# Attention times V as three passes into one PSUM bank, one group of three tiles, a second attention with P as weights, and a written-out tail

## The reference

```python
B, Q, S, D, H, DH = 8, 100, 1444, 128, 16, 64
def first(x, ctx):                       # wq, wk, wv, wo, norm_w are weights
    normed = x * rsqrt(mean(x*x, -1) + 1e-6) * norm_w
    q, k, v = heads(normed @ wq), heads(ctx @ wk), heads(ctx @ wv)
    return x + merge(softmax(q @ k.T) @ v) @ wo
def second(x1, ctx):
    return x1 + softmax(x1 @ ctx.T) @ ctx
out = second(first(x, ctx_1024), ctx_1024)
```

## Time and profile before

| what | value |
|---|---|
| median of 3 runs | 704.48 us (704.47 to 707.13) |
| span of the profiled execution | 704.5 us |
| the profiled execution's own time | 706.28 us |
| PE busy | 680.9 us (97%) |
| PE weight loads busy | 604.9 us (86%) |
| DVE busy | 484.0 us (69%) |
| ACT busy | 469.5 us (67%) |
| POOL busy | 159.9 us (23%) |
| mean granted TensorE clock | 0.985 |

### The profile page before, as it was taken

One profiled execution on the slowest core, in us unless ns is written; L12 is line 12 of the kernel. 1 busy time (PEld: TensorE's weight loads), 2 busy tenths in 40 slices (PEclk: granted clock), 3 DMA queues, 4 the chain that ended last, 5 costly groups with the idle time before them and its releaser, 6 DMA issues.

```text
span 704.5 us, 13025 instructions
## 1 busy us (share of the span) xinstructions
PE 680.9 (97%) x4424; PEld 604.9 (86%) x4424; DVE 484.0 (69%) x1074; ACT 469.5 (67%) x1176; POOL 159.9 (23%) x486
## 2 busy tenths in 40 slices
PE   5899999999999999999999999999999999999976
PEld 5688889888998898988998889988999888988965
DVE  3586567677776777677776777677776777668722
ACT  4777577677766677667766677667776677666622
POOL 2211114111231214121241213221231212312100
PEclk9999999999999999999999999999999999999995
DMA  5012112120222111221121111211112112110120
GB/s 186 1 53 16 7 11 54 9 15 9 15 53 16 15 5 19 53 15 9 7 58 14 13 12 12 58 11 15 5 18 52 15 9 15 13 11 10 11 18 3
DMA packets 27146, 16.61 MB, mean 24 GB/s; under 512 B 15786, under 2 KB 25418, under 8 KB 27082
## 3 DMA queue, kind: packets, MB, share of 16 engines
q1 hardware_dynamic: 27082, 15.79, 17.0%
HBM read 15.32 MB, written 0.46 MB: 22 GB/s over the span
## 4 chain that ended last, share of the span: by engine, by line
PE 91%; DMA 3%; ACT 3%; DVE 2%; issue 1%; SPq 0%; ACTq 0%
PE ps_o L1072 31%; PE ps_t L1020 19%; PE ps_s L989 11%; PE ps_s L993 10%; PE ps_s L990 10%; PE ps_m L1088 4%; PE ps_m L931 3%; DMA denominator_rows<-rinv 2%; PE ps_t L945 2%; ACT probs L696 1%; DMA x_rows<-in_x_dram 1%; DVE pT_both L753 1%; PE ps_s L918 1%; DMA out_dram<-result 0%; DMA rinv_row<-denominator_rows 0%
## 5 line engine op out<-in xcount | busy, mean ns | idle before, releaser
L675 ACT ACTIVATE pT_both<-ps_t 128x496 fp32r<-128x496 f32 (+1 forms) x336 | 194.4, 581 | 188.4 <-PE ps_t L1020 188.0
L1072 PE MATMUL ps_o<-pT_both,c_hi 128*128 128x496 f32 (+4 forms) x768 | 253.3, 375 | 0.0
L753 DVE TENSOR_TENSOR pT_both<-ps_t,pT_both 128x496 fp32r<-128x496 f32 (+1 forms) x336 | 202.6, 616 | 45.4 <-ACT pT_both L675 44.9
L808 DVE TENSOR_REDUCE part_max<-ps_s 124x1 f32<-124x512 f32 (+1 forms) x336 | 209.2, 650 | 23.7 <-PE ps_s L993 23.5
L696 ACT ACTIVATE probs<-ps_s,neg_max 124x512 f32<-124x512 f32 (+1 forms) x336 | 218.9, 663 | 6.9 <-DVE neg_max L815 6.9
L1020 PE MATMUL ps_t<-ident,probs 124*128 124x124 f32 (+2 forms) x1232 | 184.3, 268 | 7.2 <-DVE pT_both L753 4.9
L1020 PEld LDWEIGHTS ps_t<-ident,probs 124*128 124x128 f32 (+2 forms) x1232 | 148.6, 141 | 46.4 <-issue 9.2
L1072 PE MATMUL ps_o<-pT_both,c_lo 128*128 128x248 f32 (+3 forms) x704 | 187.0, 266 | 0.0
L1072 PEld LDWEIGHTS ps_o<-pT_both,c_hi 128*128 128x128 f32 x768 | 146.6, 191 | 14.9
L539 POOL CAST tails<-probs 124x36 fp32r<-124x36 f32 (+1 forms) x224 | 41.0, 215 | 469.2 <-ACT probs L696 373.9
L989 PE MATMUL ps_s<-cT_hi,q_hi 128*124 128x512 f32 (+3 forms) x312 | 143.9, 461 | 1.2 <-DVE q_lo L753 1.2
(11 more groups left out here) (119 smaller groups left out, 493.0 us busy)
## 6 DMA issues: line engine op xcount, KB each, us to landing
rinv_row<-denominator_rows SPq DMA_DIRECT2D x48, 124.0 KB, 3.6
ctx_raw<-in_ctx_dram SPq DMA_DIRECT2D x8, 704.0 KB
denominator_rows<-rinv SPq DMA_DIRECT2D x48, 1.0 KB
wq_sb<-in_L_xattn_wq_dram SPq DMA_DIRECT2D x2, 256.0 KB, 5.8
wk_sb<-in_L_xattn_wk_dram SPq DMA_DIRECT2D x2, 256.0 KB, 6.0
wv_sb<-in_L_xattn_wv_dram SPq DMA_DIRECT2D x1, 512.0 KB, 7.7
wo_sb<-in_L_xattn_wo_dram SPq DMA_DIRECT2D x1, 512.0 KB, 8.7
rinv_row<-denominator_rows SPq DMA_DIRECT2D x8, 62.0 KB, 3.8
```

Source lines behind the costliest of these rows:

```text
L675: act.activation(pT_both[buf][:, j0:j0 + nj, 0, col:col + m], ps_t[:, bank, 0:nj * m].rearrange("p (j m) -> p j m", m=m), ACT.Copy).then_i ...
L753: dve.tensor_tensor(dst, src, hi.bitcast(F32), ALU.subtract).then_inc(done, 1)
L808: mx = dve.tensor_reduce(part_max[0:m, s, c:c + 1], ps_s[0:m, score_bank(s, c, par), 0:CHUNKS[c][1]], AX.X, ALU.max)
L1072: t = pe.matmul(*all_[i], start=(i == 0), stop=(i == len(all_) - 1))
```

## The change

It does these things at once:

- PV of a group runs as three passes per slot, c_hi x p_hi, c_hi x p_lo and c_lo x p_hi, all of the group's own width and all accumulated into one bank region: 34 matmuls for each group. DVE multiplies it by `rinv_row` straight into `o_norm` (`take_out`); the copy on ACT, the sum on DVE and the product on POOL go.
- The groups are (0,1), (2,3), (4,5), (6,7), (8,9,10), (11,12), and the plan of PV over the steps is new.
- The late PV has the transposed exponentials as weights (100 columns) and c_hi, c_lo side by side as the moving operand; its output has queries as rows, and the transpose back goes. ACT scales one half, POOL adds the x1 rows, DVE does the rest. It runs in one piece in step 12.
- The context is split in steps 13, 0 and 1 and stacked in step 2. The projection moves from steps 2 to 5 to steps 0 to 3, the q pairs to steps 5 to 10, 12 and 13, and the first item of every batch waits for all eight pairs.
- The late item of batch 6 is taken out of batch 7, and the end is written out: it runs there beside the last PVs of batch 7. The last group's denominators are spread over the partitions by a matmul with ones against diagonal matrices instead of the way over DRAM.

The diff, cut to its core:

```diff
-    GROUPS = [(0, 1), (2, 3), (4, 5), (6, 7), (8,), (9, 10), (11, 12)]
+    GROUPS = [(0, 1), (2, 3), (4, 5), (6, 7), (8, 9, 10), (11, 12)]
-    PV_PLAN = {0: (5, -1, 1, 2), 1: (6, -1, 0, 2), 2: (6, -1, 1, 2),
-               3: (0, 0, 0, 2), 4: (0, 0, 1, 2), 5: (1, 0, 0, 2), 6: (1, 0, 1, 2),
-               7: (2, 0, 0, 2), 8: (2, 0, 1, 2), 9: (3, 0, 0, 2), 10: (3, 0, 1, 2),
-               11: (LATE, -1, 0, 1), 12: (4, 0, 0, 1), 13: (5, 0, 0, 2)}
+    PV_PLAN = {13: (4, 0, 0, 17), 0: (4, -1, 17, 34), 1: (5, -1, 0, 17), 2: (5, -1, 17, 34),
+               3: (0, 0, 0, 17), 4: (0, 0, 17, 34), 5: (1, 0, 0, 17), 6: (1, 0, 17, 34),
+               7: (2, 0, 0, 12), 8: (2, 0, 12, 23), 9: (2, 0, 23, 34),
+               10: (3, 0, 0, 17), 11: (3, 0, 17, 34)}
+    LATE_PV_STEP = 12
+    EVAC = {1: (4, -1), 3: (5, -1), 5: (0, 0), 7: (1, 0), 10: (2, 0), 12: (3, 0)}
-    PAIR_STEPS = {1: 0, 6: 1, 7: 2, 8: 3, 9: 4, 10: 5, 13: 6}
-    LAST_PAIR_STEP = 0
+    PAIR_STEPS = {5: 0, 6: 1, 7: 2, 8: 3, 9: 4, 10: 5, 12: 6, 13: 7}
-    OUT_HEADS = {2: range(0, 5), 3: range(5, 9), 4: range(9, 13), 5: range(13, 16)}
+    OUT_HEADS = {0: range(0, 5), 1: range(5, 9), 2: range(9, 13), 3: range(13, 16)}
-    CTX_SPLIT_STEPS = {12: (0, 1), 13: (1, 1), 0: (2, 0)}
-    STACK_STEP = 1
+    CTX_SPLIT_STEPS = {13: (0, 1), 0: (1, 0), 1: (2, 0)}
+    STACK_STEP = 2
...
+            for b in range(B):                                  # SP
+                if b < B - 1:
+                    sp.wait_ge(ctx_turned, n(b, NC, NC - 1))
+                    sp.wait_ge(ctx_lo_done, n(b, len(CTX_SPLIT), len(CTX_SPLIT) - 1))
+                    sp.wait_ge(stack_steps, n(b, 3, 2))
+                    load_ctx(b + 1)
+                for g in range(NG):
...
+                    sp.wait_ge(inverted, k + 1)
+                    sp.dma_start(scratch[b:b + 1, cols].rearrange("a (t p) -> p (a t)", p=TM),
...
+                    sp.wait_ge(rinv_stored, 16 * (k + 1))
...
+                    sp.dma_start(rinv_row[:, k % 2, 0:TM * count],
...
+                    if (b, s) in NUMBER:                        # POOL
+                        split_tail(NUMBER[b, s])
...
+                    if s == STACK_STEP and 0 < b:
+                        stack_tail(b)
...
+            def late_scaled(bb):                                # ACT
+                act.wait_ge(pv_done, block(bb, LATE))
...
+                act.activation(late_lo[0:Q, :], ps_o[0:Q, 0, D:2 * D], ACT.Copy,
+                               scale=rinv[0:Q, k:k + 1]).then_inc(late_lo_out, 1)
...
+            def take_out(b, g):                                 # DVE
+                k, w = NG * b + g, group_width(g)
+                dve.wait_ge(pv_done, block(b, g))
...
+                    dve.wait_ge(rinv_row_loaded[g], 16 * (b + 1))
...
+                dve.tensor_tensor(o_norm[:, group_cols(g)], ps_o[:, 0, 0:w], rinv_row[:, k % 2, 0:w],
+                                  ALU.mult).then_inc(pv_out, 1)
...
+                    if s in EVAC:
+                        grp, off = EVAC[s]
+                        if b + off >= 0:
+                            take_out(b + off, grp)
+                    if here:
+                        chunk_maximum(g, 0)
...
+                    if s == 0:                                  # PE, scores
+                        pe.wait_ge(ctxT_lo, n(b, NC, NC - 1))
+                        pe.wait_ge(q_lo_done, pairs_up_to(b - b % 2, HP - 1))
...
+            def pv(b, grp, lo, hi, by_chunk=False):
...
+                    if block(b, grp) > 1:
+                        pe.wait_ge(pv_out, block(b, grp) - 1)
+                    if grp == 0:
...
+                        pe.wait_ge(ctx_lo_done, n(b, len(CTX_SPLIT), len(CTX_SPLIT) - 1))
+                        pe.wait_ge(stack_steps, n(b, 3, 2))
+                for i in range(lo, hi):
+                    j, part = divmod(i, 3)
...
+                    weights = c2[:, j, (0, 0, 1)[part], :]
+                    moving = p[:, j, (0, 1, 0)[part], 0:w]
+                    t = pe.matmul(ps_o[:, 0, 0:w], weights, moving, start=(i == 0), stop=(i == UNITS - 1))
...
+                    pe.matmul(ps_o[0:Q, 0, 0:2 * D], pT_late[:, j, 0, :],
+                              c2[:, j, :, :].rearrange("p a d -> p (a d)"), start=(j == 0), stop=False)
+                    pe.matmul(ps_o[0:Q, 0, 0:D], pT_late[:, j, 1, :], c2[:, j, 0, :],
+                              start=False, stop=False)
...
+            last = B - 1                                        # PE, the end
+            scores(L_FIRST, 0)
+            turn(T_LAST, 0)
+            scores(L_FIRST, 1)
+            turn(T_LAST, 1)
+            scores(L_FIRST, 2)
+            pv(last, NG - 2, 17, UNITS)
+            turn(T_LAST, 2)
...
+            project(last, range(0, 9))
...
+            pv(last, NG - 1, 0, UNITS, by_chunk=True)
+            project(last, range(9, 13))
+            turn(L_FIRST, 0)
+            turn(L_FIRST, 1)
...
+            project(last, range(13, 16))
+            turn(L_FIRST, 2)
...
+                scores(L_LAST, c)
...
+            pv_late(last - 1)
+            for c in range(NC):
+                turn(L_LAST, c)
+            pv_late(last, by_chunk=True)
```

More of the change, by code:

```diff
@@ L102, in n, with block @@
+    BLOCKS += [(B - 2, LATE), (B - 1, LATE)]
+    def block(b, g):
+        return BLOCKS.index((b, g)) + 1
+    TURNS = []
+    for g, (b, s, _, _) in enumerate(ITEMS):
+        if g > 0 and g < L_FIRST:
+            TURNS += [("item", g - 1, c) for c in range(NC)]
+        if b < B - 1 and s in CTX_T_STEPS:
+            TURNS.append(("ctx", b + 1, CTX_T_STEPS.index(s)))
+    for g in (T_LAST, L_FIRST, L_LAST):
+        TURNS += [("item", g, c) for c in range(NC)]
     def n(b, per_batch, index):
@@ L303, in bass_two_cross_attentions @@
-        TURNS = []
-        for s in range(STEPS):
-            TURNS += [("item", s - 1, c) for c in range(NC)]
-            if s in CTX_T_STEPS:
-                TURNS.append(("ctx", s, CTX_T_STEPS.index(s)))
-        def turn_exists(at, first, last, nxt):
-            what, s, _ = TURNS[at]
-            if what == "ctx":
-                return nxt
-            if s < 0:
-                return not first
-            return item_exists(s, first, last)
-        def turn_bank(what, s, c, par):
-            return (len(TURNS) * par + TURNS.index((what, s, c))) % 2
@@ new lines, in wait_turn_bank, with turn @@
+            def wait_turn_bank(what, at, c):
+                k = TURNS.index((what, at, c)) - 2
+                if k >= 0:
+                    what, at, c = TURNS[k]
+                    if what == "ctx":
+                        pe.wait_ge(ctxT_lo, n(at, NC, c))
+                    else:
+                        pe.wait_ge(turned_lo, ev(at, c))
+            def turn(g, c):
+                m = rows(ITEMS[g][2])
+                pe.wait_ge(exped, ev(g, c))
+                wait_turn_bank("item", g, c)
+                if g == 0 and c == 1:
+                    pe.wait_ge(wqk_ready, 4)
+                j0, nj = TILE_SLOTS[c]
+                for j in range(j0, j0 + nj):
+                    if j < FULL:
+                        src = probs[g % 2][0:m, P * j:P * (j + 1)]
+                    else:
+                        pe.wait_ge(tail_split, g + 1)
+                        src = tails[g % 2][0:m, :]
+                    t = pe.transpose(ps_t[:, turn_bank("item", g, c), m * (j - j0):m * (j - j0 + 1)], src,
+                                     ident[0:m, 0:m])
+                t.then_inc(turned, 1)
@@ new lines, in _ @@
+            for b in range(B):
+                for s in range(STEPS):
+                    here = (b, s) in NUMBER
+                    g = NUMBER.get((b, s))
+                    prev = item_before(b, s)
+                    part = pv_of(b, s)
+                    for c in range(NC):
+                        if here:
+                            scores(g, c)
+                        if prev is not None and c < NC - 1:
+                            turn(prev, c)
+                    mid = None
+                    if part is not None:
+                        bb, grp, lo, hi = part
+                        mid = lo + (hi - lo) // 2
+                        pv(bb, grp, lo, mid)
+                    if prev is not None:
+                        turn(prev, NC - 1)
+                    if part is not None:
+                        pv(bb, grp, mid, hi)
+                    if s == LATE_PV_STEP and 0 < b < B - 1:
+                        pv_late(b - 1)
+                    misc(b, s)
+                    if s in CTX_T_STEPS and b < B - 1:
@@ new lines, in _ @@
+            last = B - 1
[6 more added lines that the diff above has]
+            turn(T_LAST, 2)
+            pe.wait_ge(x1_rows_ready, last)
+            wait_heads(last, range(0, 9))
+            project(last, range(0, 9))
+            pe.wait_ge(diag_made, 2)
+            col = 0
+            for i, t in enumerate(GROUPS[NG - 1]):
+                m = rows(t)
```

(3 more changed lines are left out.)

1131 lines of the change are left out of this document (511 added, 620 removed).

## The result

The changed kernel takes 742.3 us (median of 4 runs, 739.6 to 744.5), the kernel before in the same session 705.3 us (704.5 to 707.1): a ratio of 1.053, with an interval from 1.051 to 1.055. The forecast was 719 us with a range from 700 to 728. The direction was right; the loss is 37 us where 14.5 were forecast.

A forecast was written before the change was run, and what follows sets the result against it. PE was taken as the bound, busy for 97% of the span. 704.5 - 5.0 (PV) + 10.1 (stack) + 13.2 (DMA) + 4.2 (pair 7) - 8.1 (end) = 718.9, say 719 us, range 700 to 728.

The forecast's parts named there:

- The DMA term: Group (0,1) denominators, stored behind the late context load, make PE wait before PV (2,3) in six batches: +13.2 us.
- three waits: New PE waits: stack before PV (0,1), 7 times; DVE's product behind the DMA, 6 times; pair 7, 3 times.
- PV on PE: PV and late PV in new passes save about 0.5 and 0.25 us a batch: -5.0 us.
- The rival of slow passes: Passes of 248 and 236 columns run at 0.125 us: 15 us more, 734 us; chance 0.06.
- the rule on loads: Skill's rule: weight loads overlap only across row groups, so 43 added loads a batch cost in full: 758 us; chance 0.01.
- The stack: Context's rest, stacked in step 2, is late for PV (0,1) in step 3: 1.4 us in batches 1 to 7, +10.1.
- Pair 7: First scores of batches 2, 4 and 6 wait for the last q pair: 1.4 us each, +4.2 us.
- The end: Written-out end of 33.5 us, 0.4 for batch 7's step 12, and a shorter batch 7: -8.1 us.
- The gain without waits: Rival: stack, row and pairs are all in time, so no wait arises: 691 us; chance 0.14.
- The row in time with the stack late: Rival: the stack is late but the DMA isn't, with a store of 5 to 6 us: 706 us; chance 0.09.

The follow-up runs named there:

- the kernel without the three waits: Changed kernel with the stack back in step 1, tiles waiting only for needed q pairs, and group (0,1) denominators stored and loaded before the next context: 700.6 us.
- the run with the product first: Kernel with all three waits removed, and DVE at the end taking out the last group before the late item's first two low parts: 698.2 us, ratio 0.989.
- the one with the row first: Changed kernel, but SP waits until the row of group (0,1) has landed before storing group (1)'s denominators: 745.5 us, ratio 1.055.

## Why the prediction was right or wrong

Two steps failed. The DMA term had the row's landing and the cost behind a wait too small: 26 us where it had 13.2. And the new plan was put at nothing away from its three waits, while each batch takes 0.5 us more instead of 0.75 less: +3 where the sum had -5.0. The three waits themselves, their places and their numbers (7, 6 and 3) came as forecast.

- **PV on PE (-5.0).** The prices of the passes inside a piece hold: 0.115 and 0.170 us, and the group of three takes 6.0 us where (8) and (9,10) took 6.7. The rival of slow passes (734) and the rule on loads (758) fall. But the gain did not arrive. In the kernel without the three waits, an even batch takes 79.75 us, before 79.71, though it also has one q pair less to do (0.54); an odd one 84.49 against 83.42, with one pair more. The mean is 0.5 us more a batch, not 0.75 less. By kind of work, counted by distances from start to start, PV and late PV gained 0.3 a batch where 0.65 were forecast, since a group of two costs 0.06 to 0.16 us more in its new pieces. Small stalls took 0.9: 0.2 to 0.3 us each before the third transposes of step 12 and before PV of step 13, 0.2 at other transposes, all behind scores, 0.4 in an even batch ahead of the context's transposes, and 0.1 among the transposes. The step that failed was to cost the new plan at nothing away from its three waits. For batch 7's step 12 I had put 0.4; a like gap was in the other six. Stalls and pieces together are 1.25 a batch, some 8 us of the result.
- **The stack (+10.1).** Right: 9.4 us of waits, 1.58 us a batch from the length of step 3, 11 us in all.
- **The DMA (+13.2).** The mechanism was right and its size wrong: 26 us. Two terms of it were mis-sized. The wait was 2.7 us in the mean and up to 4.7, not 1.9, since the row landed 3.8 to 6.3 us after its issue, 4.8 in the mean, and I had taken the median of the earlier trace rows, 3.6 over all groups. The store (7.1 in the mean, 7.2 taken) and PE's way to the product (11.25 us in batch 5, 11.2 taken) were right. And the consequence of a wait was 0.3 us only in batch 4; in the other five it was 1.6 to 1.9, with the granted clock at 0.50 for about 3 us. I had put the lower clock into the end only, though the earlier trace rows already showed what it does to a PE that waits.
- **Pair 7 (+4.2).** 1.6 us three times, 4.8.
- **The end (-8.1).** From the start of batch 7 to the end of the span it was 111.8 us before and is 108.2 after. Without the stack's 1.58 that is -5.2, and the PV that moved out of the first batch gives another -1.4: -6.6. The written-out end takes 34.3 us, where 33.5 were forecast. Its steps are where I had put them up to the late PV of batch 6 (the last heads at 15.65 against 15.5, the last item's scores at 17.8 against 17.4); behind that it takes 16.6 us where 16.1 were forecast, with the granted clock at 0.50 from 25.3 us to the end; that the 1.5 us put in for the lower clock were too few is likely, not shown. The wait before the last heads was in the sum; the run with the product first shows that it need not be there.
- **The first batch (not in the sum).** It starts 0.5 us earlier and is 3.3 us shorter than the moved PV explains. Before, PE waited 1.03 and 0.92 us there for low parts of the transposes, and ran at a clock of 0.50 from 90 to 93 us; neither recurs. That these are the 3.3 us is argued from their sizes, and no run tries it. I had read no row of it.
- **The rivals.** The gain without waits was worked out as 691, 13.1 us under the kernel before; the kernel without them takes 700.6, 5.2 under it in its session, mainly since the batches didn't get shorter. The row in time with the stack late was worked out as 706; that kernel takes 716.3, mainly for the same reason.

The sum with measured prices: 704.5 + 3 (PV and stalls, six batches of 0.5) + 11 (stack) + 26 (DMA) + 4.8 (pairs) - 6.6 (end) - 3.8 (first batch) = 738.9, against a span of 739.2 us. Part of the error was hidden by luck: the 3.3 us of the first batch are a gain that no term forecast.

## What to carry to other kernels

Price a wait of TensorE by what it does to the clock too: here each wait of 1.8 to 4.7 us came with about 3 us at half the clock, and cost 1.6 to 1.9 us more than itself; the one of 1.1 us did not. Before a small transfer is put behind a large one on the same queue, look for who waits at its end, and whether an engine that had slack there has just been replaced by one that hasn't: here one line of order on SP was worth 26 us, and some 8 with the stack early. And a plan that saves work on the bound engine has to be read for new gaps of 0.2 us between all its steps, and for what more pieces cost; together they were more in a batch (1.25 us) than the work it was to save (0.75).

## What was not expected of the hardware

- A store of 1 KB, with the wait for it, takes 4.9 to 6.7 us by itself (changed kernel and the one with the row first), and 6.5 to 10.1 right behind a load in the changed kernel and its variants, with the DMA engines at a share of 0.00 for the last 3 to 7 us of it. In the kernel before the difference doesn't stand out (5.0 to 8.4 and 6.2 to 8.4).
- A load of 124 KB that follows such a store lands after 3.4 to 5.4 us or, in some batches, after 5.8 to 8.6. The spread between executions of a kernel that waits for it was 4 to 9 us, and 0.3 to 3.0 us in those that don't.
- After 4.85 us without work, the granted clock is still 1.00 when PE starts and falls to 0.50 only 0.3 us later, for about 3 us. Behind the waits of 1.8 and 2.2 us it falls 1.6 and 0.9 us after PE's start.
